# Indirect row scatters spread over more attention units, with moved statistics, a later choice of experts for one batch and an earlier weight split

## The reference, cut to what matters

```python
x = x + xattn0(layernorm(x), ctx)          # scores of 512 x 512, normed, softmax
x = x + ffn0(layernorm(x))                 # Hadamard, 8-bit tokens, ternary weights
x = x + xattn1(layernorm(x), ctx, ctx)     # 32 query heads, 8 key heads, head width 16
x = x + moe(layernorm(x))                  # 8 experts, the best 2 of each token

# moe
logits = x @ gate_w
top_logits, top_idx = top_k(logits, 2)
top_w = softmax(top_logits)
for e in range(8):
    h = silu(x @ w0[e]) * (x @ w1[e])
    out += cw[:, e:e+1] * (h @ wo[e])
```

## Time and profile before

| | |
|---|---|
| three runs | 1662.42, 1666.59, 1664.45 us; median 1664.45 us |
| profiled execution | 1672.16 us, its span 1670.3 us |
| PE busy | 1567.2 us, 94% of the span |
| DVE busy | 948.0 us, 57% |
| ACT busy | 717.6 us, 43% |
| POOL busy | 702.1 us, 42% |
| phase C | about 493 to 918 us of the span |
| phase D up to the first expert product | 918 to 950 us |

### The profile page before, as it was taken

One profiled execution on the slowest core, in us unless ns is written; L12 is line 12 of the kernel. 1 busy time (PEld: TensorE's weight loads), 2 busy tenths in 40 slices (PEclk: granted clock), 3 DMA queues, 4 the chain that ended last, 5 costly groups with the idle time before them and its releaser, 6 DMA issues.

```text
span 1670.3 us, 24439 instructions
## 1 busy us (share of the span) xinstructions
PE 1567.2 (94%) x8124; PEld 1047.5 (63%) x8150; DVE 948.0 (57%) x1539; ACT 717.6 (43%) x1160; POOL 702.1 (42%) x479
## 2 busy tenths in 40 slices
PE   6869999999889999999899899999999999999998
PEld 4555657565543434434333778788788888788886
DVE  6998979796878897887885622222122222222221
ACT  5885646455547777777677211111111111111111
POOL 1124251633513125254354765670862180930064
PEclk9889999999898999999999999999999999999999
DMA  9189800000231445243430625231440140530088
GB/s 357 56 305 386 291 1 1 0 1 1 84 94 47 123 132 149 82 126 111 148 114 28 224 70 189 82 120 32 182 176 26 59 155 26 188 127 26 26 140 213
DMA packets 90944, 196.16 MB, mean 117 GB/s; under 512 B 7153, under 2 KB 9074, under 8 KB 90226
## 3 DMA queue, kind: packets, MB, share of 16 engines
q1 hardware_dynamic: 71746, 156.68, 28.2%
q0 software_dynamic: 7168, 17.04, 4.5%
q10 hardware_dynamic: 11952, 21.43, 3.9%
HBM read 113.28 MB, written 81.32 MB: 117 GB/s over the span
## 4 chain that ended last, share of the span: by engine, by line
PE 68%; DVE 16%; POOL 6%; ACT 4%; issue 3%; DMA 3%; another core or an unknown queue 0%; SPq 0%; POOLq 0%; DVEq 0%; ACTq 0%
PE psum L2929 11%; PE psum L2931 11%; PE psum L2930 11%; PE psum L2580 6%; DVE neg_max L2057 5%; PE psum L2782 5%; PE psum L2771 5%; PE psum L2744 4%; POOL expert_weight_parts L1052 3%; PE psum L2625 3%; PE psum L2595 2%; DMA w_of_even_expert<-in_L_ffn_w 2%; PE psum L2953 2%; POOL expert_weight_parts L1051 1%; DVE inner_rotated_t_second L1926 1%
## 5 line engine op out<-in xcount | busy, mean ns | idle before, releaser
L2057 DVE TENSOR_REDUCE neg_max<-psum 128x2 f32<-128x1024 f32 x248 | 291.3, 1220 | 49.5 <-PE psum L2744 48.3
L1420 ACT ACTIVATE probabilities<-psum 128x512 f32<-128x512 f32 x512 | 271.7, 601 | 85.2 <-PE psum L2771 81.3
L2199 DVE TENSOR_TENSOR expert_inner<-psum,expert_inner 128x512 f32<-128x512 f32 x78 | 53.9, 692 | 388.7 <-ACT expert_inner L1526 378.6
L2929 PE MATMUL psum<-expert_weight_parts,sorted_tokens_t_first 128*128 x624 | 250.8, 402 | 8.8 <-POOL expert_weight_parts L1052 5.1
L2930 PE MATMUL psum<-expert_weight_parts,sorted_tokens_t_first 128*128 x624 | 246.8, 396 | 0.0
L2931 PE MATMUL psum<-expert_weight_parts,sorted_tokens_t_second 128*128 x624 | 246.8, 395 | 0.0
L1526 ACT ACTIVATE expert_inner<-psum 128x512 f32<-128x512 f32 x78 | 46.7, 599 | 396.7 <-PE psum L2931 396.7
L2771 PE MATMUL psum<-query_rows,key_rows 50*128 50x512 f32 x512 | 179.3, 444 | 4.1 <-ACT probabilities L1420 3.0
L2744 PE MATMUL psum<-key_rows,query_rows 48*128 48x512 f32 x496 | 170.6, 491 | 11.7 <-DVE neg_max L2057 5.8
L2929 PEld LDWEIGHTS psum<-expert_weight_parts,sorted_tokens_t_first 128*128 128x128 f32 x624 | 117.7, 189 | 37.4 <-issue 11.1
L2782 PE MATMUL psum<-probabilities,value_and_one 128*32 128x512 f32 x1024 | 140.3, 620 | 0.8 <-ACT probabilities L1420 0.7
(11 more groups left out here) (316 smaller groups left out, 2924.3 us busy)
## 6 DMA issues: line engine op xcount, KB each, us to landing
sorted_x<-zero_rows SPq DMA_DIRECT2D x9, 3960.0 KB, 30.5
w_of_odd_expert<-in_L_ffn_w SPq DMA_DIRECT2D x8, 2048.0 KB
wo_of_expert<-in_L_ffn_wo SPq DMA_DIRECT2D x7, 2048.0 KB, 8.6
query_rows<-query_rows_of_units SPq DMA_DIRECT2D x64, 192.0 KB, 3.5
w_of_even_expert<-in_L_ffn_w SPq DMA_DIRECT2D x6, 2048.0 KB, 11.6
sorted_tokens<-sorted_x ACTq DMA_DIRECT2D x39, 264.0 KB, 2.8
sorted_y<-expert_out ACTq DMA_DIRECT2D x39, 256.0 KB
query_rows_of_units<-dims_first SPq DMA_DIRECT2D x32, 256.0 KB
```

Of the source, the lines that this page charges most:

```text
L1420: nc.scalar.activation(prob[t % 2][:, i * SEQ:(i + 1) * SEQ], bank[4 + n % 3], ACT.Exp, scale=HD ** -0.5).then_inc(c_e, 1)
L2057: nc.vector.tensor_reduce(of_pair[:, p, st, :], ring(("max", (m, i))).rearrange("p (h n) -> p h n", h=2), AX.X, ALU.max, negate=True).then ...
L2199: nc.vector.tensor_tensor(h, bank[2 * half + 1], h, ALU.mult).then_inc(e_h, 1)
L2929: nc.tensor.matmul(out_bank, hi[:, cols], w_r[:, bass.ds(w_at, 512)], start=start, stop=False)
```

## The change

It does seven things. (1) The scatters of batches 0 and 1 are issued by a table: batch 0 one token tile (two DMAs) in each of units 15 to 18, batch 1 one tile in units 23 and 24 and two tiles in unit 25; batch 2 stays at two tiles in units 30 and 31. (2) The statistics of batch 3 move from between units -1 and 0 to behind units 3 and 4, their deviation behind unit 5. (3) For batch 2, parts 1 to 5 of the choice all stand at (30, 0), and the rank is at (30, 2). (4) The four pieces of the first expert's w0 are loaded in units 26 and 27. (5) Both halves of its w1 are split on POOL in unit 29, none in unit 30 or in phase D. (6) In phase D the first two parts of batch 3's choice go ahead of `shift`. (7) Six unread identity products follow the transposes of the first expert tile.

```diff
         ROUTED_AT = {0: 11, 1: 19, 2: 26}
+        SCATTERED_AT = {15: (0, (0,)), 16: (0, (1,)), 17: (0, (2,)), 18: (0, (3,)), 23: (1, (0,)), 24: (1, (1,)), 25: (1, (2, 3)),
+                        30: (2, (0, 1)), 31: (2, (2, 3))}
...
-            routing_jobs[(u_ + 4, 1)] = [("rank", b_)]
+            routing_jobs[(u_ + 4, 2 if b_ == BATCH - 2 else 1)] = [("rank", b_)]
...
-                if u in (25, 26):
+                if u in (26, 27):
                     sp.wait_ge(*scattered(0))
                     sp.wait_ge(*scattered(1))
-                    first_expert(2 * (u - 25))
-                    first_expert(2 * (u - 25) + 1)
+                    first_expert(2 * (u - 26))
+                    first_expert(2 * (u - 26) + 1)
...
-                        scatter(b, 0)
-                    if routing(u, 5) is not None:
-                        scatter(routing(u, 5), 1)
+                    if u in SCATTERED_AT:
+                        scatter(*SCATTERED_AT[u])
...
-                    if u == UNITS - 2:
-                        half_split(w_in_raw[0][1], W_IN[0][1], 0, w_in_parts, 0)
+                    if u == 29:
+                        for h in range(2):
+                            half_split(w_in_raw[0][1], W_IN[0][1], h, w_in_parts, h)
...
                 last_scatters()
-                half_split(w_in_raw[0][1], W_IN[0][1], 1, w_in_parts, 1)
...
-                    if routing(u, 3) is not None:
+                    if routing(u, 3) is not None and routing(u, 3) < BATCH - 2:
                         choose(routing(u, 3), t + 1)
                     if t == 0 and routing(u, 4) is not None:
-                        choose(routing(u, 4), 5)
+                        for part in range(1 if routing(u, 4) == BATCH - 2 else 5, 6):
+                            choose(routing(u, 4), part)
...
+                if u in (3, 4):
+                    tokens_statistics(BATCH - 1, u - 1)
+                if u == 5:
+                    queries_deviation(BATCH - 1)
...
                 b = BATCH - 1
+                choose(b, 0)
+                choose(b, 1)
                 dve.wait_ge(r_rstd, BATCH)
...
-                for part in range(6):
+                for part in range(2, 6):
                     choose(b, part)
...
                 attention(-1)
-                tokens_statistics(BATCH - 1, 2)
-                tokens_statistics(BATCH - 1, 3)
-                queries_deviation(BATCH - 1)
...
                         last.then_inc(e_htr, 1)
+                    if static(i) and i == 0:
+                        unread(6, bank[7])
```

More of the change, by code:

```diff
@@ L509, in network @@
             routing_jobs[(u_ + 2, 2)] = [("pick", b_)]
-            routing_jobs[(u_ + 4, 1)] = [("rank", b_)]
+            routing_jobs[(u_ + 4, 2 if b_ == BATCH - 2 else 1)] = [("rank", b_)]
         routing_jobs[(UNITS - 2, 0)] = [("router sums", None)]
-        routing_jobs[(UNITS - 2, 2)] = [("x dims", 0)]
+        routing_jobs[(UNITS - 2, 2)].append(("x dims", 0))
         routing_jobs[(UNITS - 2, 3)] = [("x dims", 1)]
@@ L942, in batch_rows, with scatter @@
                 nc.gpsimd.tensor_copy(rows[1], rows[0]).then_inc(d_dup, 1)
-            def scatter(b, half):
-                if b == 0 and half == 0:
+            def scatter(b, tiles_of_batch):
+                if b == 0 and tiles_of_batch[0] == 0:
                     pool.wait_ge(d_zf, 16 * (ZEROED + 1))
@@ L951, in scatter @@
                 pool.wait_ge(d_dup, b + 1)
-                for st in (2 * half, 2 * half + 1):
+                for st in tiles_of_batch:
                     t = b * ST + st
@@ L1434, in attention @@
                         logits_out(routing(u, 2))
-                    if t == 1 and routing(u, 4) is not None:
+                    if routing(u, 4) is not None and t == (2 if routing(u, 4) == BATCH - 2 else 1):
                         rank_out(routing(u, 4))
```

## The result

| | before | the change |
|---|---|---|
| median of the runs | 1663.82 us (1662.42 to 1666.59, 4 runs) | 1682.09 us (1679.90 to 1684.14, 4 runs) |
| ratio, 95% interval | | 1.0111 [1.0095, 1.0127] |
| profiled execution, its span | 1672.16, 1670.3 us | 1681.58, 1679.7 us |
| unit 17, unit 24 | 16.61, 15.83 us | 13.22, 11.37 us |
| first L2753 of unit 30 (L2758 now) to the first expert transposes | 52.92 us | 67.15 us |

The forecast was 1661.1, the result is 21 us above it and 18.3 above before. Lines of the changed kernel stand higher than before: L2753 is L2758, L2812 is L2817, L2151 is L2157, L2057 is L2058; POOL's split, L1051 and L1052 before, is L1052 and L1053.

A forecast was written before the change was run, and what follows sets the result against it. It took PE, holding 68% of the chain that ended last, as the bound. Terms summed to -3.3 us against the profiled 1672.16, giving 1668.9, or 1661.1 against the median; range 1654.5 to 1667.5 us.

The forecast's parts named there:

- The scatters: Units 17 and 24: spreading the scatters saves half of the time lost by ACT and DVE standing still, -3.8 us.
- The wait at (30, 2): Unit 30: DVE's choice products wait for POOL's split, so PE goes on 3.4 us late; bounds 0 and 4.5.
- The clock behind it: Behind PE's gap at (30, 2): the granted clock falls, costing 1.6 us; bounds 0 and 2.
- The clock at the start: Around unit 0: the clock rises some 2.8 us earlier in PE's work, gaining 1.4 us; bounds 0 and 2.6.
- The start: Before unit 0: taking out batch 3's statistics gives PE 1.8 us; bounds 0 and 1.8.
- the statistics put back: Behind units 3, 4 and 5: batch 3's statistics fall on DVE with little slack, costing 0.8 us.
- Unit 29: Unit 29 loses eight small DVE instructions of batch 2's choice, gaining 0.5 us; bounds 0 and 0.8.
- the loads: Units 26 and 27: the pieces of w0 go out a unit later, with no effect, 0 us.
- Phase D: Phase D: with POOL's split gone, ACT's rows and everything behind them come 1.3 us earlier; bounds 0.5 and 2.
- The fill: Before the second expert tile: six unread products gain 0.3 us; bounds 1.5 gained and 1.5 lost.
- The sum's base: Whole kernel: -3.3 us from the profiled 1672.16 gives 1668.9; that execution lies 7.7 above the median, so 1661.1.
- The slower rival: Unit 25: its row of four scatters adds a stand-still of 4.15 us, two others kept; 1669.1 us, chance 0.07.

The follow-up runs named there:

- second trace: The kernel before, unchanged, profiled once more: 1664.97 us, span 1663.1 us.
- wait_filled_short: The changed kernel with 12 unread identity products on PE ahead of the rank's wait at (30, 2): 1670.46 us, ratio 1.0039.
- wait_filled: The changed kernel with 22 unread identity products on PE ahead of the rank's wait at (30, 2): 1674.89 us, ratio 1.0067.
- late_choice_one_half: The kernel before with batch 2's choice at (30, 0), rank at (30, 2), w1's first half split in unit 29, second in phase D: 1660.52 us, ratio 0.9988.
- mended: late_choice_one_half plus unread products in units -1 and 0 and six behind the first expert tile: 1662.82 us, ratio 0.9996.
- choice_back: The changed kernel with batch 2's choice back in unit 29 and its rank at (30, 1), both w1 splits left in unit 29: 1676.73 us, ratio 1.0081.

## Why the prediction was wrong, step by step

Three steps make most of the 21 us. The largest is the price of the low clock behind the wait, +1.6 us forecast with a bound of 2, 11.9 measured: 10.3 us. Next come the scatters, -3.8 forecast and +1.8 in the trace, 5.6 us, and the clock at the start, -1.4 forecast and +2.5 in the trace, 3.9 us.

- *The scatters, -3.8 us.* It took half of two stand-stills from one execution as if the common run had them, though the text itself said that this execution lay 7.7 us above the median and that the stand-stills were 7.7 us. The second trace has none. The spread gained nothing against the median, and cost 1.8 us in the trace through units 25 and 26 (3.1 by the medians); I had only feared a stand-still from their row of four, and called the moved scatters free on POOL.
- *The wait at (30, 2), +3.4.* Right in place and kind, 3.01 measured. The products that met the copy and the subtraction stood two and three places further along the chain than I had them: POOL's second copy began together with the chain (890.37 and 890.36), where I had it 0.5 us ahead, and the chain's first product passed in 0.17 us. SBUF — State Buffer, "Who interferes with whom", in the Trainium skill, says that a DVE instruction with two SBUF inputs and a GpSimd one that reads SBUF block each other; this case agrees with it (1.55 and 4.24 us here, 4.05 and 4.34 with the choice in unit 29). The same section says that `tensor_scalar` can contend too, if its operands meet certain conditions. That would fit `var_eps_all`, 0.83 us; no run here tried it.
- *The clock behind it, +1.6, bounds 0 and 2.* The worst step: 11.9 us (wait_filled_short). I took the price of the fall from unit 17 and did not ask what PE does behind the wait. Units 30 and 31 have no row maxima, and unit 17 has; but the changed kernel's clock also stayed low from 500 to 516 us, with PE busy and row maxima in its work, so it is not shown that their absence is the reason.
- *The clock at the start, -1.4, bounds 0 and 2.6.* Wrong sign: +2.5 in the trace. With the statistics gone PE is busy from 500 us on but for 0.45 us, and the clock still rose later, at 516. I let it rise with the time of work, and the trace gave no such rule. Why it rises later is open; it does not in every execution.
- *The start, -1.8, and the statistics put back, +0.8.* -1.6 (the wait itself 0.45 us instead of 1.82) and +1.3, the latter in all nine traces with the moved statistics: mechanism right, the second one undersized. The part as a whole, a gain of 2.4 us by its terms, lost 4.3 when it was run alone.
- *Unit 29, -0.5, and the loads, 0.* -0.6 in unit 29; units 27 and 28 took 29.08 us together, as before (29.09).
- *Phase D, -1.3.* Not seen in the change, as the logits came at the low clock. Where it was high (wait_filled), 13.65 us from the attended transposes to the last scatters against 14.86 (15.06 to 15.41 in the other traces whose POOL and choice stand as before): -1.2 to -1.8. Without part 6 (late_choice_one_half) 12.83. So part 6 seems to take back 0.8, though the same code in mended took 14.33 us, as the clock was low there.
- *The fill, -0.3.* The gap ahead of the second tile is gone (0.23 us), and the products cost nothing beside the loads. The tile was 1.5 us shorter than in the second trace of before, but as short in five traces without the fill; alone it did not show in the median.
- *The sum's base.* The sum went from the trace to the median by taking off 7.7 us, which are the two stand-stills, and took off 3.8 for them once more as a term. A term that undoes what only the trace has must not be set against the median; without it the sum is 1664.9.

Units 13 and 14, +1.4, were in no step: a fall of the clock at 676 us, which two of the traces have and the others not; four others of the changed kernel and its variants have one in unit 18 instead, 1.3 to 1.4 us. The slower rival (one more stand-still) had the right unit (25) for a small part of the loss, and the wrong mechanism; no rival joined the wait to the stretch behind it.

## What to carry to other kernels

Before a term is drawn from a stall, ask whether the traced execution is a common one: where it lies above the median by as much as the stall, take a second trace. Price a wait on TensorE together with the work that follows it: a 3 us gap ahead of two units without row maxima cost 15 us, and the same gap filled with products nobody reads cost 3 (the wait itself). Two-input work on VectorE and long work on GpSimd need places in the order that do not touch; here one half split less in the unit was the difference between 14 us slower and a kernel that is at least no slower than before (3 us faster by the medians, not clear of noise). And before a gain is put down to an edit, look for traces without the edit that have it too.

## What the runs showed of the hardware

- The granted clock stayed at 0.50 from 899 to 929 us with PE shown busy in most of it, and was back at 1.00 behind six identity products in phase D, or twelve in unit 30. In the second trace of before, with the same work and no gap, it was at 1.00 from 884 to 905 us; in choice_back it was low for 20 us of this work and came back without identity products.
- With one gap filled there was often a fall at another; whether the filling moved it is not shown, as falls change place between executions. At an idle wait a fall is cheap when products nobody reads follow it (3.56 us of wait, then `unread(10)`); on the first expert tile it cost 1.5 to 2.7 us.
- ACT and DVE stood still together in one trace of eighteen, the first of before. Its cause was not tried. Another trace (late_choice_one_half) has a late load of maxima in unit 17, 1.74 us of wait on PE, and a fall behind it.
- A single-input DVE instruction waited for a POOL subtraction as well (0.83 against 0.17 us), in all seven traces with a row of four scatters in unit 25, and in none of the eleven without.
